# Gated cross-attention and routed layer: one pass that gives the softmax shift, and an opening that prepares the weights part by part

## The reference

```
lat = layer_norm(layernorm(x), g_l, b_l)         # 112 x 256
ctx = layer_norm(ctx, g_m, b_m)                  # 375 x 256
q   = lat @ Wq                                   # 16 heads x 64
k,v = split(concat(ctx, lat) @ Wkv)              # 487 rows, 16 heads x 64
p   = softmax(q k^T / 8)                         # 112 x 487 in each head
x2  = x + tanh(g_x) * (concat_heads(p v) @ Wout)
out = x2 + tanh(g_f) * experts(layernorm(x2))    # 8 experts, the best 2 of each row
```

## Time and profile before

| | |
|---|---|
| median of 3 runs | 1902.32 us (1900.02 to 1903.77) |
| the profiled execution, its own time | 1902.62 us |
| its span | 1900.9 us |
| TensorE busy | 1674.2 us, 88% |
| VectorE busy | 1428.0 us, 75% |
| ScalarE busy | 1195.3 us, 63% |
| GpSimd busy | 1183.0 us, 62% |

### The profile page before, as it was taken

One profiled execution on the slowest core, in us unless ns is written; L12 is line 12 of the kernel. 1 busy time (PEld: TensorE's weight loads), 2 busy tenths in 40 slices (PEclk: granted clock), 3 DMA queues, 4 the chain that ended last, 5 costly groups with the idle time before them and its releaser, 6 DMA issues. The chain is left out here.

```text
span 1900.9 us, 42714 instructions
## 1 busy us (share of the span) xinstructions
PE 1674.2 (88%) x15031; PEld 1163.1 (61%) x15032; DVE 1428.0 (75%) x2917; ACT 1195.3 (63%) x2666; POOL 1183.0 (62%) x1297
## 2 busy tenths in 40 slices
PE   2899999999999999999999999998402999999980
PEld 1456666666666666666666666665302999989970
DVE  4777888888888888888888888877395666666646
ACT  2587777777777777877777777777254333433320
POOL 4477777777777777777777777767263343333320
PEclk9999999999999999999999999999555999999995
DMA  3267766767767666676776776767455111111119
GB/s 131 46 127 140 142 144 131 139 139 142 147 129 145 138 140 144 135 139 138 139 150 136 136 137 129 138 130 142 118 186 173 46 49 45 50 50 47 47 35 289
DMA packets 599541, 233.18 MB, mean 123 GB/s; under 512 B 534064, under 2 KB 584016, under 8 KB 598992
## 3 DMA queue, kind: packets, MB, share of 16 engines
q1 hardware_dynamic: 592656, 212.67, 52.5%
q0 software_dynamic: 6720, 18.36, 3.1%
HBM read 78.66 MB, written 20.19 MB: 52 GB/s over the span
## 5 line engine op out<-in xcount | busy, mean ns | idle before, releaser
L279 POOL TENSOR_TENSOR p_parts<-p_f,p_parts 112x487 f16<-112x487 f32 x512 | 560.4, 1118 | 194.2 <-ACT p_parts L374 194.2
L365 ACT ACTIVATE p_f<-scores_ps,shift 112x487 f32<-112x487 f32 x512 | 337.0, 663 | 13.3 <-DVE shift L500 9.7
L495 DVE TENSOR_REDUCE neg_max<-scores_ps 112x1 f32<-112x487 f32 x512 | 313.0, 654 | 27.1 <-PE scores_ps L653 27.1
L402 ACT ACTIVATE k_hi<-proj_ps 128x488 fp32r<-128x488 f32 x256 | 147.9, 578 | 262.5 <-PE proj_ps L635 262.5
L1018 ACT ACTIVATE space<-h_ps,b_sb,undo 128x256 f32<-128x256 f32 x280 | 142.8, 560 | 232.1 <-PE h_ps L1247 228.8
L374 ACT ACTIVATE p_parts<-p_f 112x487 f16<-112x487 f32 x512 | 275.9, 607 | 0.0
L536 DVE SCALAR_TENSOR_TENSOR v_sb<-proj_ps,v_sb 128x512 f16<-128x512 f32 (+1 forms) x256 | 176.5, 689 | 92.1 <-ACT v_sb L416 89.4
L530 DVE TENSOR_TENSOR k_lo<-proj_ps,k_hi 128x488 fp32r<-128x488 f32 x256 | 168.2, 657 | 78.2 <-ACT k_hi L402 78.0
L684 PE MATMUL pv_ps<-v_sb,pt_sb 128*128 128x128 f16 x2048 | 218.9, 221 | 7.8 <-DMA pt_sb<-p_parts 7.8
L635 PE MATMUL proj_ps<-kv_hi,wkv_hi 128*128 128x488 f16 x512 | 192.3, 376 | 22.0 <-POOL kv_lo L306 13.5
L635 PE MATMUL proj_ps<-wkv_hi,kv_hi 128*128 128x512 f16 (+1 forms) x512 | 194.6, 380 | 0.1
(11 more groups left out here) (222 smaller groups left out, 4075.1 us busy)
## 6 DMA issues: line engine op xcount, KB each, us to landing
w_part<-in_L_ffn_w_dram SPq DMA_DIRECT2D x64, 256.0 KB, 3.5
stage<-in_L_ffn_w_dram SPq DMA_DIRECT2D x32, 512.0 KB, 4.1
ctx_sb<-in_ctx_dram SPq DMA_DIRECT2D x32, 375.0 KB
space<-y_rows SPq DMA_DIRECT2D x32, 224.0 KB, 4.7
pt_sb<-p_parts SPq DMA_TRANSPOSE x256, 4.0
x_sb<-in_x_dram SPq DMA_DIRECT2D x32, 112.0 KB
res_sb<-in_x_dram SPq DMA_DIRECT2D x32, 112.0 KB, 5.3
x_dram<-x_sb SPq DMA_DIRECT2D x32, 112.0 KB, 2.9
```

The source lines that it names most:

```text
L279: pool.tensor_tensor(p_parts[0:LQ, p % PS, h, 1, 0:LK], p_f[0:LQ, p % 2, h, 0:LK], p_parts[0:LQ, p % PS, h, 0, 0:LK], ALU.subtract).then_i ...
L365: act.activation(p_f[0:LQ, p % 2, h, 0:LK], scores_ps[n][0:LQ, 0:LK], ACT.Exp, bias=shift[0:LQ, p // 2 % 2, n:n + 1], accum_out=row_sum[0: ...
L402: act.activation(k_hi[:, j], ps[:, 0:LKP], ACT.Copy).then_inc(kq_high, 1)
L495: dve.tensor_reduce(neg_max[0:LQ, p // 2 % 2, n:n + 1], scores_ps[n][0:LQ, 0:LK], AX.X, ALU.max, negate=True).then_inc(max_done, 1)
```

## The change

**The shift.** The scale that takes the powers of two out of Q gets a minus sign, so the scores come out negated. One VectorE pass per head adds P_SHIFT to all 487 columns, writes the result as float16 to a tile `passed` that nobody reads, and gives the minimum of it per row as the shift; ScalarE computes exp(-score + shift). The negated maximum and the bias are gone, and ScalarE waits for each head's shift by itself.

**The opening.** wkv is loaded in four column chunks (first half of K, first half of V, second half of K, second half of V), each with its own semaphore, now into `p_parts`' space; wout goes into `pt_sb`'s. The small loads move to ScalarE's queue. One chain of scales becomes four: layer-norm vectors (VectorE t = -24 and -22), wkv (t = -22), wq (maximum at t = -11, the rest at -8 and -6), wout (-4, -3, -2). The weights are split in seven turns: wkv's first two chunks before K and V start, the other chunks, wq's halves and wout between steps -8 and 0. TensorE waits for each where it first needs it. GpSimd's memsets of `p_parts` move to t = -1, that of `pt_sb` to t = 1; SP's first transpose waits for wout's low part.

The diff, cut to its core:

```diff
-        stage = v_flat[:, 0:KD * 2 * INNER].rearrange("p (k n) -> p k n", k=KD)
+        stage = p_parts[:, :, :, :, :].rearrange("p s h a n -> p (s h a n)").bitcast(F32).rearrange("p (k n) -> p k n", k=KD)
-        stage_out = v_flat[:, KD * 3 * INNER:KD * 3 * INNER + NP * D].rearrange("p (j n) -> p j n", j=NP)
+        stage_out = pt_sb[:, :, :].rearrange("p s n -> p (s n)").bitcast(F32)[:, 0:NP * D].rearrange("p (j n) -> p j n", j=NP)
+        KV_CHUNKS = (0, INNER, CHUNK, INNER + CHUNK)
+        W_TURN = {"kv0": 1, "kv1": 2, "kv2": 3, "q0": 4, "kv3": 5, "q1": 6, "out": 7}
...
 sync
+            for n in range(4):
+                sp.dma_start(kv_chunk(stage, n), kv_chunk(wkv.rearrange("(k p) n -> p k n", p=128), n)).then_inc(w_loaded[n], 16)
...
+                    if p == 0:
+                        sp.wait_ge(w_ready, W_TURN["out"])
 gpsimd
-            for s in range(PS):
-                pool.memset(p_parts[0:LQ, s, :, :, LK:512], 0.0).then_inc(pool_step, 1)
+            pool.memset(v_sb[96:128, 0, KT - 1], 0.0).then_inc(v_cleared, 1)
...
                 if t == -1:
-                    pool.wait_ge(w_ready, 4)
+
+                    pool.wait_ge(w_ready, W_TURN["q1"])
...
+                    for s in range(PS):
+                        pool.memset(p_parts[0:LQ, s, :, :, LK:512], 0.0).then_inc(parts_cleared, 1)
...
+                if t == 1:
+                    pool.wait_ge(w_ready, W_TURN["out"])
+                    pool.memset(pt_sb[:, :, 16 * LQ:], 0.0).then_inc(parts_cleared, 1)
 scalar
+            for n, a in enumerate((ln_m_g, ln_m_b, ln_l_g, ln_l_b)):
+                act.dma_start(affine[:, n, :], a.rearrange("(k p) -> p k", p=128), allow_slow_non_contiguous=True).then_inc(small_loaded, 16)
...
-                act.activation(p_f[0:LQ, p % 2, h, 0:LK], scores_ps[n][0:LQ, 0:LK], ACT.Exp, bias=shift[0:LQ, p // 2 % 2, n:n + 1],
+                act.activation(p_f[0:LQ, p % 2, h, 0:LK], scores_ps[n][0:LQ, 0:LK], ACT.Exp, bias=shift[0:LQ, p // 2 % 2, n:n + 1], scale=-1.0,
...
+                if t == -2 * NP + 2:
+                    weight_high("kv0")
+                    weight_high("kv1")
...
+                for turn, at in (("kv2", -8), ("q0", -6), ("kv3", -6), ("q1", -4), ("out", -1)):
+                    if t == at:
+                        weight_high(turn)
 vector
+            def shifted_minimum(p, h):
                 n = 2 * (p % 2) + h
                 dve.wait_ge(scores_done, 2 * p + h + 1)
-                dve.tensor_reduce(neg_max[0:LQ, p // 2 % 2, n:n + 1], scores_ps[n][0:LQ, 0:LK], AX.X, ALU.max, negate=True).then_inc(max_done, 1)
-
-            def bias(p):
-                n = 2 * (p % 2)
-                dve.wait_ge(max_done, 2 * p + 2)
-                dve.tensor_scalar(shift[0:LQ, p // 2 % 2, n:n + 2], neg_max[0:LQ, p // 2 % 2, n:n + 2], P_SHIFT, None, ALU.add).then_inc(bias_done, 1)
+                dve.tensor_scalar(passed[0:LQ, n], scores_ps[n][0:LQ, 0:LK], P_SHIFT, None, ALU.add, ALU.min,
+                                  accum_out=shift[0:LQ, p // 2 % 2, n:n + 1]).then_inc(shift_done, 1)
...
+                if t == -3 * NP:
+                    input_peaks()
                 if t == -3 * NP + 2:
-                    weight_scales()
+                    input_scale()
+                    kv_scale()
                 if t == -NP - 3:
-                    split_kv_weights()
...
+                    weight_low("kv0")
+                    weight_low("kv1")
+                    q_peak()
...
+                for turn, at in (("kv2", -7), ("q0", -5), ("kv3", -5), ("q1", -3), ("out", 0)):
+                    if t == at:
+                        weight_low(turn)
+                if t == -8:
+                    largest(2, 1, 2)
+                if t == -6:
+                    q_scale()
+                if t == -4:
+                    out_peak()
+                if t == -3:
+                    largest(3, 2, 3)
+                if t == -2:
+                    out_scale()
 tensor
-                            pe.wait_ge(w_ready, 2)
+                            pe.wait_ge(w_ready, W_TURN["kv1"])
+                    if b == -1 and j == 4:
+                        pe.wait_ge(w_ready, W_TURN["kv3"])
...
-                    if b == -1 and n == 0:
-                        pe.wait_ge(w_ready, 3)
+                    if b == -1:
+                        pe.wait_ge(w_ready, W_TURN[f"q{n}"])
```

More of the change, by code:

```diff
@@ new lines, in power @@
+            def power(turn, first, last):
+                at = slice(first, last)
+                dve.wait_ge(peaks_moved, 4 * turn + 4)
+                then(dve.tensor_copy(peak_e[:, at], tail_ps[:, 128:128 + last - first]))
+                if turn == 0:
+                    then(dve.scalar_tensor_tensor(out=peak_e[:, 3:4], in0=peak_e[:, 3:4], scalar=16.0, in1=peak_e[:, 4:5], op0=ALU.mult, op1=ALU.add))
+                    at = slice(3, 4)
+                then(dve.tensor_scalar(exponent[:, 0, at], peak_e[:, at].bitcast(I32), 23, None, ALU.arith_shift_right))
+                then(dve.tensor_scalar(exponent[:, 1, at], exponent[:, 0, at], -1.0, 268.0, ALU.mult, ALU.add))
+                then(dve.tensor_scalar(exponent[:, 2, at], exponent[:, 1, at], 156.0, None, ALU.min))
+                then(dve.tensor_scalar(exponent[:, 3, at], exponent[:, 2, at], -1.0, 254.0, ALU.mult, ALU.add))
+                then(dve.tensor_scalar(scale_i[:, :, at], exponent[:, 2:4, at], float(2 ** 23), None, ALU.mult))
@@ new lines, in kv_scale @@
+            def kv_scale():
+                for n in range(4):
+                    dve.wait_ge(w_loaded[n], 16)
+                    last = dve.tensor_reduce(peak_kv[:, n:n + 1], kv_chunk(stage, n), AX.XY, ALU.max, apply_absolute_value=True)
+                then(last)
+                then(dve.tensor_reduce(peak[:, 0:1], peak_kv[:, :], AX.X, ALU.max))
+                dve.sem_inc(peaks_moved, 1)
+                largest(1, 0, 1)
+                power(1, 0, 1)
+                dve.sem_inc(scales_ready, 1)
@@ L520, in _ @@
                 if t % 2 == 0 and is_pair(t):
-                    maximum(t, 0)
-                    maximum(t, 1)
-                    maximum(t + 1, 0)
-                    bias(t)
-                    maximum(t + 1, 1)
-                    bias(t + 1)
+                    for p in (t, t + 1):
+                        for h in range(2):
+                            shifted_minimum(p, h)
                 if is_pair(t + NP):
@@ L611, in _, with turn_peaks, spread_peaks @@
             pe.wait_ge(set_up, 1)
-            pe.wait_ge(peaks_moved, 1)
-            nc.tensor.transpose(tail_ps[0:5, 0:128], peak[:, :], ident[:, :]).then_inc(peaks_moved, 1)
-            pe.wait_ge(peaks_moved, 3)
-            nc.tensor.matmul(tail_ps[:, 128:133], ones[0:5, :], peak_diag[:, :], start=True, stop=True).then_inc(peaks_moved, 1)
+            def turn_peaks(turn, first, last):
+                pe.wait_ge(peaks_moved, 4 * turn + 1)
+                nc.tensor.transpose(tail_ps[0:last - first, 0:128], peak[:, first:last], ident[:, :]).then_inc(peaks_moved, 1)
+            def spread_peaks(turn, first, last):
+                pe.wait_ge(peaks_moved, 4 * turn + 3)
+                nc.tensor.matmul(tail_ps[:, 128:128 + last - first], ones[0:last - first, :], peak_diag[0:last - first, first:last],
+                                 start=True, stop=True).then_inc(peaks_moved, 1)
+            for turn, first, last in ((0, 3, 5), (1, 0, 1)):
+                turn_peaks(turn, first, last)
+                spread_peaks(turn, first, last)
             def take(kind, index):
```

153 lines of the change are left out of this document (82 added, 71 removed).

## The result

The changed kernel takes 1888.13 us in the median (1886.58 to 1888.43), the kernel before, measured with it, 1902.03 (1900.02 to 1903.77). The ratio is 0.9925, 95% interval 0.9910 to 0.9941. The forecast was 1886. The total came out near because two errors cancelled: the shift brings more than forecast, and the opening, which was to gain 0.7 us and lose 2 by the clock, costs 6.8 us.

What follows compares the result with a forecast made beforehand. TensorE, busy 98.9%, was taken as the bound. Shift 16.8, first batch 1.0 and opening 0.7, less 2.0 for the clock, gave 16.5 us off 1902.6: 1886, range 1874 to 1899.

Steps and rivals of the forecast that it cites:

- signs of being wrong: Read over 0.15 us between passes, TensorE waiting for another tile instead, or first scores later than 75 us.
- sign of being right: In the steady stretch, TensorE's idle time was to fall from 9.2 us in 840 to 3 or less.
- the first hole: TensorE's wait before the transpose and next K at a fourth step: closes by 0.24 us a batch, limited by `v_lo`.
- the second bias: VectorE's last bias before `k_lo`: takes 0.39 us because it waits for what the maximum in front wrote.
- The read: VectorE's read of the running minimum after each pass: 0.09 us, with no wait on a semaphore.
- The second such K of a batch: TensorE's other K projection waiting for `k_lo`, assumed like the one after step six: 0.17 us closes.
- The opening's head start: Before K: scales near 21 us, K near 31 instead of 40.35, a gain of 9.3 us.
- The ring: TensorE, ScalarE, VectorE loop from K to first scores, 32.9 us: inserted work costs 6.6 and 2.0 us.
- the read costs something, 0.19 or 0.39 us: Minimum's read on VectorE: at 0.19 us near 1900, chance 0.12; at 0.39 us slower, near 1975 at worst, chance 0.05.
- rival (b): Read waits 0.39 us for its pass, delaying TensorE through `k_lo`: 77 us, near 1975 at worst; chance 0.05.
- the opening keeps 7 to 9 us: Most insertions before the first scores lie in VectorE's idle time and the clock stays up: 1878; chance 0.23.
- rival (d): Opening is a loss, holes and half clock costing 6 us more than thought: 1892; chance 0.12.

Runs made afterwards that it cites:

- the run with four instructions: Kernel after the change, each pass replaced by a plain reduction to the minimum straight into the shift, without the added constant: 1887.23 us.
- The one with five (one bias): Kernel before the change, four maxima in a row and one bias over four columns behind them instead of two biases: 1980.52 us, ratio 1.0407.
- two orders changed: Kernel after the change, wkv's maxima and chain ahead of the small loads', batch 1's statistics and normalization moved behind batch 0's work: 1880.76 us.
- wkv's chain first: Kernel after the change, wkv's maxima and scale chain ahead of the small loads' on VectorE and TensorE: 1884.48 us.
- the statistics first: Kernel after the change, the maxima of the small vectors moved behind batch 0's statistics on VectorE: 1886.55 us.
- the pass alone: Kernel before the change with the additive running-minimum pass and nothing of the new opening: 1881.33 us, ratio 0.9889.

## Why the prediction was right, and where it was not

**The direction and the time** were right: 16.5 us forecast, 13.9 measured. That the time is so near is luck: the shift was forecast 3 to 4 us too low and the opening 5.5 us too high. Two of the forecast's own signs of being wrong came in. TensorE waits for `v_lo`, as the sum itself had it for one hole, and the first scores come later than 75 us. Its sign of being right, TensorE's idle time at 3 us or less, did not: it is 6.9.

**The shift**, forecast at 16.8 us over 29 batches and 1.0 in the first, is 20.8 over 30 intervals and 1.3 in the first batch (29.0 to 27.6 us from the scores to the first `peaks`). The path is the one forecast, through `k_lo` to TensorE, and the first hole closes by 0.25 us where 0.24 was said, held by `v_lo`. One reason was wrong and changed no term: the second bias was said to take 0.39 us because it waits for what the maximum in front of it wrote. With the same wait and GpSimd idle it adds 0.07 us (77.16 to 77.23), and the wait itself 0.12 in front of it (76.46 to 77.16 is 0.70, where maxima follow each other in 0.58); the rest is GpSimd's. Three sizes were off. The read was put at 0.09 us a head and costs nothing; this changed no hole, since `v_hi` holds that place anyway, as the run with four instructions shows. "The second such K of a batch I take as equal" was not read from the trace: its hole closed by 0.23 instead of 0.17. And the two batches with a 38.6 us period got 1.1 us each, not 0.58; why twice as much, no run tells.

**The Trainium skill's** count of operations ("VectorE: DVE Perf Modes", Rules for kernel authors) was set against the trace in the forecast, and the trace was right to be followed: eight instructions beat six, and cost what four cost. The one with five (one bias) is the slowest of all. An order of instructions that others wait for is not priced by its number.

**The opening's head start** is the step that failed: "scales near 21", "K starts near 31", 9.3 us in all. The saving of 4.4 us for wq's and wout's maxima was there, but the small chain "done by then" was not. It waited until 12.4 us for the small vectors, and batch 0's statistics waited behind it on VectorE; then the rest of the chain, from 14.48 on, cost 4.1 us, with two tiny steps of 1.09 and 0.54 us where 0.17 and 0.23 are normal. wkv's maxima started at 18.59 instead of 13.4, 5.2 of the 5.4 us missed. Splitting only half of wkv ahead of K, with the `undo` arithmetic behind it, saved 3.7 us where 3.8 was said. The runs show the head start to be real: with two orders changed K starts at 28.76.

Those two tiny steps ran beside GpSimd's normalization; with wkv's chain first they came when GpSimd had finished, and took 0.17 and 0.23. In the kernel after they end at 17.98 and 18.56, two of GpSimd's instructions at 17.96 and 18.54. With the statistics first the stall moves to two other steps, 0.99 and 1.19 us long, which end at 13.83 and 15.95, 0.02 us behind GpSimd's again. Not every small step stalls: those at 16.52 and 16.70, over one column, ran beside GpSimd and took 0.15. The Trainium skill ("SBUF — State Buffer", Who interferes with whom) says that VectorE and GpSimd lock each other out at a shared port, that a `tensor_scalar` can take it, and that an instruction of VectorE with two inputs in SBUF contends with GpSimd's reads. The traces agree, for the biases and the steps as above, and in the other direction: `kv_lo` takes 1.10 us alone and 3.39 beside the low parts of wkv, 5.52 beside whole ones.

**The ring** was forecast to lose 6.6 + 2.0 us, and 2 by the clock: 10.6. Measured: 41.8 - 32.9 = 8.9, and 1.2 more in the first batch, where wout's low part now lies (28.8 us with the new opening, 27.6 with the old one, both with the pass). The falls of the clock within the ring are 3.4 of it by the windows row; the slow start behind K's wait is about 1.0 shorter, so the clock's share is near 2.4. The sum was good. Against the opening's own gain of 3.9 that leaves the first scores 5.0 us later, where 1.3 was forecast.

**The rivals.** That the read costs something, 0.19 or 0.39 us, fell with the first timeline. The run with one bias lost 77.6 us, and 77 was the price of rival (b), but that is chance: the rival's delay went over a late `k_lo`, and in that run `k_lo` is hardly later (3.25 us against 3.18). There the delay goes over ScalarE's order and `v_lo`, which the forecast did not have. That the opening keeps 7 to 9 us fell; that it is a loss, rival (d), is what happened. The shift's surplus hid it.

The routed part took 539.4 us after, 538.4 with the pass alone and 537.6 before. No line of it is touched, and no run tells why.

## What to carry to other kernels

In an opening, look for what the first matmul waits for last, and put what belongs to a later batch behind it. Here, work that was moved from ahead of the ring into it made holes there, and behind the largest of them TensorE ran at half the clock. When a small instruction produces what another engine waits for, its place counts as well as its price: ask when the first consumer can start, not how many instructions there are. Where a small VectorE instruction takes longer than its like, compare its end with the ends of GpSimd's instructions. Measure the parts of a double change one by one; here one part's surplus paid for the other's loss.

## What the runs showed that was not expected

- VectorE's accumulator read takes 0.08 us and starts together with the next pass. With it a pass over 112 x 487 from PSUM with a float16 result has the spacing of a plain maximum, 0.58 to 0.59 us, and lasts 0.659 us in the mean against 0.654.
- A bias over two columns took 0.16 us where GpSimd was idle, 0.40 in the mean of the steady stretch, and 1.06 in the first batch, and the long ones end with an instruction of GpSimd. Of the 0.84 us that the pass saves between the first read of the scores and `k_lo` in the step shown, 0.63 are of this kind (3.18 less 2.55).
- One bias fewer made the kernel 78 us slower.
- Six loads of 0.5 to 8 KB, issued from ScalarE's queue ahead of all else, landed after 5.0 to 10.1 us beside the large ones on SP's queue.
